# The change of x2 from token rows to feature rows for batches 2 to 5: TensorE turns replaced by 32 by 32 block turns and transfers

## What is computed

```python
x = _layernorm(x + _L0_attn_ref(x, Wq, Wk, Wv, Wo))      # causal self-attention, 16 heads, rotary
x = _layernorm(x + _L0_xattn_ref(x, ctx_4096))           # softmax(x ctx^T) ctx
x = _layernorm(x + _L0_ffn_ref(x, weight, bias, lora_A, lora_B, lora_start_indices))  # x W^T + bias + LoRA by batch
```

## Time and profile before

| | before |
|---|---|
| median of 3 runs (lowest, highest) | 523.33 us (523.15, 524.16) |
| the profiled execution, its own time | 522.58 us |
| its span, first to last instruction | 520.6 us |
| PE busy | 513.0 us, 99% of the span |
| PEld, DVE, ACT, POOL busy | 438.4, 319.8, 262.6, 152.1 us |
| granted TensorE clock, mean | 0.996 of full speed |
| DMA, all 16 engines | 65.60 MB, mean 126 GB/s |

### The profile page before, as it was taken

How to read it: one execution, slowest core, us unless ns; L and a number is a source line. 1 busy time by engine, 2 the same in 40 slices (tenths; PEclk the granted TensorE clock), 3 DMA queues, 4 the chain that set the end, 5 groups by cost and what they waited for, 6 DMA issues and landing times.

```text
span 520.6 us, 7823 instructions
## 1 busy us (share of the span) xinstructions
PE 513.0 (99%) x2864; PEld 438.4 (84%) x2864; DVE 319.8 (61%) x693; ACT 262.6 (50%) x664; POOL 152.1 (29%) x139
## 2 busy tenths in 40 slices
PE   8999999999999999999999999999999999999995
PEld 5888888888989888888978888888887888988884
DVE  5822000187776868677674797769887776845432
ACT  5713210183856648384565356357868464525231
POOL 0003500536353554742006150113937000110010
PEclk9999999999999999999999999999999999999998
DMA  8907612331021111100095677579987477333011
GB/s 284 320 16 180 184 40 82 126 118 51 32 69 55 42 40 43 42 2 0 1 280 162 146 205 210 148 200 262 263 247 212 133 207 214 104 91 110 1 75 47
DMA packets 37958, 65.60 MB, mean 126 GB/s; under 512 B 4872, under 2 KB 20616, under 8 KB 37920
## 3 DMA queue, kind: packets, MB, share of 16 engines
q1 hardware_dynamic: 37248, 64.58, 43.1%
q10 hardware_dynamic: 672, 0.52, 0.3%
HBM read 54.08 MB, written 3.67 MB: 111 GB/s over the span
## 4 chain that ended last, share of the span: by engine, by line
PE 98%; DMA 1%; ACT 0%; DVE 0%; SPq 0%; issue 0%; ACTq 0%
PE bank L539 30%; PE bank L656 30%; PE bank L550 15%; PE bank L742 6%; PE bank L566 3%; PE bank L581 3%; PE bank L773 2%; PE bank L775 2%; PE bank L778 2%; PE bank L726 1%; PE bank L715 1%; DMA x_raw<-x_feat 1%; PE bank L687 1%; PE bank L793 1%; PE bank L689 1%; PE bank L796 1%
## 5 line engine op out<-in xcount | busy, mean ns | idle before, releaser
L539 PE MATMUL bank<-x_hi,w_hi 128*128 128x512 f32 (+1 forms) x256 | 93.7, 366 | 0.0
L539 PE MATMUL bank<-x_hi,w_lo 128*128 128x512 f32 (+1 forms) x256 | 93.2, 364 | 0.0
L539 PE MATMUL bank<-x_lo,w_hi 128*128 128x512 f32 (+1 forms) x256 | 93.1, 364 | 0.0
L1386 DVE STREAM_TRANSPOSE prob_t<-prob 32x256 f32<-32x256 f32 x160 | 69.7, 436 | 12.1 <-ACT prob L947 9.4
L656 PE MATMUL bank<-wo,act_hi 128*128 128x512 f32 x224 | 70.2, 395 | 0.0
L656 PE MATMUL bank<-ffn,act_hi 128*128 128x512 f32 x224 | 70.0, 394 | 0.0
L1755 POOL TENSOR_TENSOR w_lo<-w_mix,w_hi 128x1024 fp32r<-128x1024 f32 x16 | 38.3, 2396 | 104.6 <-ACT w_hi L922 104.6
L937 ACT ACTIVATE prob<-prob,shift 112x112 f32<-112x112 f32 x128 | 47.8, 378 | 40.8 <-DVE shift L1369 40.8
L1768 POOL TENSOR_TENSOR norm<-norm,minus_half 128x1 f32<-128x1 f32 (+1 forms) x22 | 16.8, 765 | 156.5 <-DVE norm L1459 156.5
L539 PEld LDWEIGHTS bank<-x_hi,w_hi 128*128 128x128 f32 x256 | 48.1, 188 | 6.0
L539 PEld LDWEIGHTS bank<-x_lo,w_hi 128*128 128x128 f32 x256 | 48.1, 188 | 5.1
(11 more groups left out here) (119 smaller groups left out, 960.6 us busy)
## 6 DMA issues: line engine op xcount, KB each, us to landing
cf_raw<-ctx_feat SPq DMA_DIRECT2D x32, 376.0 KB, 4.1
ct_raw<-ctx_tok SPq DMA_DIRECT2D x24, 448.0 KB
w_raw<-qkv_w SPq DMA_DIRECT2D x16, 512.0 KB, 3.4
half_raw<-wo_w SPq DMA_DIRECT2D x16, 256.0 KB, 5.8
half_raw<-ffn_w SPq DMA_DIRECT2D x16, 256.0 KB, 7.0
wv_raw<-qkv_w SPq DMA_DIRECT2D x15, 256.0 KB, 7.2
x_raw<-x_feat SPq DMA_DIRECT2D x7, 448.0 KB, 8.1
out<-y_t SPq DMA_DIRECT2D x6, 512.0 KB, 3.9
```

The costliest lines, as they stand in the source:

```text
L539: last = pe.matmul(to[:, 0:cols.stop - cols.start], a[:, k, :], b[:, k, cols], start=(k == 0 and b is x_hi and a is w_hi[w]), stop=(k == K ...
L1386: return dve.transpose(quads(prob_t_wide[r], key, query), quads(prob_wide[r], query, key))
```

## The change

Batches 2 to 5 (`BLOCKS`) no longer pass through PE and PSUM. `swap_blocks(b)`: one DVE transpose of the whole row buffer in place, 128 partitions by 1024, which turns each 32 by 32 block by itself. `move_blocks(b, q)`: for 32 tokens (q = 0 to 3) four SP transfers, each of 32 partitions by 8 runs of 32 floats (16 for q = 3), carry the blocks to their feature partitions in `act_raw`, which lies on `act_lo`; four calls a batch make 16 transfers of 32 KB or less. `round_blocks(b)` on ACT waits for all 16 and writes `act_hi`, `rest_blocks(b)` on DVE writes `act_lo` in place. The row buffers get 16 rows more (112 to 127), set to zero once by POOL (`rows_set`) before the first `copy_row`. The order of the calls on SP, ACT, DVE and POOL is rewritten around this. Eight semaphores of `wv_in` become two, so `round_wv(1, k)` waits for four loads at a time.

```diff
-TURNS = ["a0", "a1", "a2", "b0", "a3", "b1", "a4", "b2", "a5", "b3", "a6", "b4", "b5", "b6", "b7"]
+TURNS = ["a0", "a1", "a2", "b0", "a3", "b1", "a4", "a5", "a6", "b6", "b7"]
+BLOCKS = range(2, 6)
...
+        act_raw = at("act_raw", [P, KT, B * S], A0 + 28672)
...
-        row = [at(f"row{i}", [S, D], (Q0 + 24576, S0 + 12288, S0 + 16384)[i]) for i in range(ROWS)]
+        row_all = [at(f"row{i}", [P, D], (Q0 + 24576, S0 + 12288, S0 + 16384)[i]) for i in range(ROWS)]
+        row = [r[0:S, :] for r in row_all]
...
             def copy_row(b, which):
                 if b >= ROWS:
-                    sp.wait_ge(turned, 2 * AT_TURN[f"b{b - ROWS}"] + 2)
+                    if b - ROWS in BLOCKS:
+                        sp.wait_ge(moved, 256 * blocks_before(b - ROWS) + 256)
+                    else:
+                        sp.wait_ge(turned, 2 * AT_TURN[f"b{b - ROWS}"] + 2)
...
+            def move_blocks(b, q):
+                sp.wait_ge(swapped, blocks_before(b) + 1)
+                if blocks_before(b):
+                    sp.wait_ge(moved, 256 * blocks_before(b))
+                t, n = b * S + QUAD * q, min(QUAD, S - QUAD * q)
+                for d in range(QUADS):
+                    sp.dma_start(act_raw[QUAD * d:QUAD * d + QUAD, :, t:t + n],
+                                 row_all[b % ROWS][QUAD * q:QUAD * q + QUAD, :].rearrange(
+                                     "p (k d i) -> p k d i", k=KT, d=QUADS)[:, :, d, 0:n]
+                                 ).then_inc(moved, 16)
...
             def ffn(i, n, turns=0):
...
+                if i + 1 in BLOCKS:
+                    pe.wait_ge(block_rest, 2 * blocks_before(i + 1) + 2)
+                else:
+                    pe.wait_ge(turn_rest, 2 * AT_TURN[f"b{i + 1}"] + 2)
...
-            turn_row(2)
-            turn_row(3)
-            turn_row(4)
-            turn_row(5)
...
+            def round_blocks(b):
+                act.wait_ge(moved, 256 * blocks_before(b) + 256)
+                for c in range(2):
+                    ks = slice(4 * c, 4 * c + 4)
+                    act.activation(act_hi[:, ks, tokens_of(b)], act_raw[:, ks, tokens_of(b)],
+                                   ACT.Copy).then_inc(block_rounded, 1)
...
+            def swap_blocks(b):
+                dve.wait_ge(x2_ready, b + 1)
+                dve.transpose(row_all[b % ROWS][:, :], row_all[b % ROWS][:, :]).then_inc(swapped, 1)
+            def rest_blocks(b):
+                for c in range(2):
+                    ks = slice(4 * c, 4 * c + 4)
+                    dve.wait_ge(block_rounded, 2 * blocks_before(b) + c + 1)
+                    dve.tensor_tensor(act_lo[:, ks, tokens_of(b)], act_raw[:, ks, tokens_of(b)],
+                                      act_hi[:, ks, tokens_of(b)].bitcast(F32),
+                                      ALU.subtract).then_inc(block_rest, 1)
```

More of the change, by code:

```diff
@@ L243, in build @@
         x_rounded, x_rest = sem("x_rounded"), sem("x_rest")
-        wv_in = [[sem(f"wv_in{c}_{k}") for k in range(KT)] for c in range(2)]
+        wv_in = [[sem(f"wv_in0_{k}") for k in range(KT)], [sem(f"wv_in1_{h}") for h in range(2)]]
         wv_rounded, wv_rest = sem("wv_rounded"), sem("wv_rest")
@@ L327, in load_wv @@
                              qkv_w[4 * c:4 * c + 4, 2, :, k, :].rearrange("s p f -> p s f")
-                             ).then_inc(wv_in[c][k], 16)
+                             ).then_inc(wv_in[0][k] if c == 0 else wv_in[1][k // 4], 16)
             def load_w(s, w):
@@ L458, in _ @@
             load_x(6)
+            load_ff(0)
+            load_ff(1)
             load_cf(14)
+            load_ff(2)
+            load_ff(3)
             load_ct(2, 0)
@@ L462, in _ @@
             load_ct(2, 2)
-            load_ff(0)
-            load_ff(1)
-            load_ff(2)
-            load_cf(15)
-            load_ff(3)
-            load_cf(16)
             load_ff(4)
-            load_cf(17)
-            copy_row(4, 0)
             load_ff(5)
@@ L474, in _ @@
             load_ff(7)
+            load_cf(15)
+            load_cf(16)
+            load_cf(17)
+            copy_row(4, 0)
             copy_row(4, 1)
@@ L480, in _ @@
             load_ff(8)
+            load_ff(9)
+            load_ff(10)
             load_cf(19)
-            load_ff(9)
+            load_ff(11)
+            move_blocks(2, 0)
+            move_blocks(2, 1)
+            move_blocks(2, 2)
+            move_blocks(2, 3)
+            load_ff(12)
             load_cf(20)
+            load_ff(13)
             load_cf(21)
-            load_ff(10)
+            load_ff(14)
+            load_cf(22)
+            load_ff(15)
             copy_row(5, 0)
             copy_row(5, 1)
-            load_ff(11)
-            load_ff(12)
-            load_ff(13)
-            load_ff(14)
-            load_ff(15)
-            load_cf(22)
             load_ct(4, 0)
@@ L499, in _ @@
             load_cf(25)
+            move_blocks(3, 0)
+            move_blocks(3, 1)
+            move_blocks(3, 2)
+            move_blocks(3, 3)
+            load_cf(26)
             copy_row(6, 0)
-            copy_row(6, 1)
-            load_cf(26)
             load_ct(5, 0)
@@ L505, in _ @@
             load_ct(5, 2)
-            store_y(0)
+            copy_row(6, 1)
             load_cf(27)
+            move_blocks(4, 0)
+            move_blocks(4, 1)
+            move_blocks(4, 2)
+            move_blocks(4, 3)
             load_cf(28)
             load_cf(29)
+            load_cf(30)
             copy_row(7, 0)
-            store_y(1)
-            load_cf(30)
+            store_y(0)
             load_ct(6, 0)
@@ L924, in round_wv @@
             def round_wv(c, k):
-                act.wait_ge(wv_in[c][k], 16)
+                if c == 0:
+                    act.wait_ge(wv_in[0][k], 16)
+                else:
+                    act.wait_ge(wv_in[1][k // 4], 64)
                 act.activation(wv_hi[c][:, k, :], wv_raw[c][:, k, :], ACT.Copy).then_inc(wv_rounded, 1)
@@ L1153, in _ @@
             cross_exp(2)
+            round_ff(0)
+            round_turned("a3")
             round_cf(14)
-            round_turned("a3")
+            round_ff(1)
+            round_ff(2)
+            round_ff(3)
             round_ct(12)
@@ L1221, in _ @@
             cross_exp(5)
-            norm_y(0)
+            round_blocks(3)
             round_cf(26)
@@ L1254, in _ @@
             round_ct(41)
+            round_blocks(5)
             cross_exp(7)
@@ L1646, in _ @@
             rest_cf(18)
+            swap_blocks(2)
             rest_ct(18)
@@ L1710, in _ @@
             rest_ct(41)
+            rest_blocks(5)
             add_row(6)
@@ L1807, in _ @@
                 rest_wo(q)
+            pool.wait_ge(heads_done, 2 * PAIRS)
+            pool.wait_ge(wo_rest, 2 * NB)
+            for i in range(ROWS):
+                pool.memset(row_all[i][P - QUAD:P, :], 0.0).then_inc(rows_set, 1)
+                pool.wait_ge(rows_set, i + 1)
             power(0, 0, P)
@@ L1813, in _ @@
             power(0, 3, P)
-            power(1, 1, S)
             add_one(0)
@@ L1828, in _ @@
             rest_ff(7)
+            power(0, 5, P)
             power(1, 2, S)
```

154 lines of the change are left out of this document (81 added, 73 removed).

## The result

| | before | after |
|---|---|---|
| median of 6 runs (lowest, highest) | 523.24 us (522.48, 524.16) | 533.28 us (530.55, 535.66) |
| the profiled execution, its own time | 522.58 us | 534.34 us |
| its span | 520.6 us | 532.3 us |
| granted TensorE clock, mean | 0.996 | 0.992 |

The change makes the kernel slower: ratio 1.0193, 95% interval 1.0164 to 1.0222, or +10.0 us by the medians. The forecast was 528.2 with a range up to 533.0, so the direction was right, the size half of what came, and the range was missed by 0.3 us.

The account below looks back on a forecast made before the run. The prediction took PE, busy 99% of the span, to bound the kernel. Its terms, -3.1 + 2.7 + 0.8 + 1.3 + 3.2 = +4.9, gave 527.5 us profiled and 528.2 as median, with a range from 520.0 to 533.

Parts of the forecast that it names:

- The removal: Four `turn_row` calls leave PE, 0.70 us each plus 0.07 for the pair behind: -3.1 us.
- the four priced stalls: PE waits forecast at `ffn(1, 0)`, `add_low(0, 0)`, `cross_score(6)` and `ffn(3, 0)`: +2.7, +0.8, +1.3 and +3.2 us.
- Price of the chain: From first move issue to finished batch: 9.9 issuing on SP, 3.0 landing, 1.75 rounding and rest; 14.65 us.
- `ffn(1, 0)`: Batch 2 moved from 382.0, finished at 396.65, while PE arrives at 393.97: a new stall of +2.7 us.
- The earlier `load_ff(0)` to `(7)` are covered by PE's own work: Loads moved ahead cost nothing; if uncovered, `norm_x2(1)` is late for `turn_row(1)` by a microsecond or so.
- `add_low(0, 0)`: `keep_t_part(0)` on ACT stands behind `round_cf(22)`, whose load the moves delay: +0.8 us, anything from 0 to 2.
- `cross_score(6)`: On DVE `rest_blocks(3)` holds back `add_row(4)` and `rest_turned("a6")`, which PE needs there: +1.3 us.
- `ffn(3, 0)`: Batch 4 moved from 431.4, finished at 446.05, while PE wants it at 442.8: +3.2 us.
- The clock: Rival: PE's clock falls to half level after stalls of 2.7 and 3.2 us, 1.5 us each: 531, chance 0.08.
- the cheap issue: Rival: SP issues each move in 0.38 us like a load, PE waits nowhere: 520.2 us, chance 0.22.
- The transfer bound: Rival: transfers themselves limit; at 60 ns a run, 15.4 us a batch and about 538 us, chance 0.05.
- its doubled case: Transfers over 32 partitions reach only 8 of 16 ports, doubling 41 ns a run: 21 us a batch, some 550 us.

Follow-up runs that it names:

- Run 1: Changed kernel's order on every queue, but no blocks: batches 2 to 5 turned on PE again; 524.74 us, ratio 1.0034 to the kernel before.
- run 3: Changed kernel with 8 moves a batch in place of 16, half of x2's features left out; 522.45 us, ratio 0.9991 to the kernel before.
- run 9: Changed kernel with 9 and 12 idle matmuls ahead of `add_low(0, 0)` and `ffn(3, 0)`; 531.74 us, ratio 1.0168 to the kernel before.
- run 5: Changed kernel with each batch's 16 moves replaced by four stores to DRAM and one load; 525.71 us, ratio 1.0050 to the kernel before.
- run 7: Changed kernel with `keep_t_part(0)` on ACT put ahead of `round_cf(21)` and `round_cf(22)`; 532.75 us, ratio 1.0186 to the kernel before.
- run 2: Changed kernel, blocks kept, with SP, ACT, DVE and POOL order from `load_x(6)` to `load_cf(17)` as before; 533.25 us, ratio 1.0192 to the kernel before.
- run 10: Changed kernel with four stores and one load through DRAM a batch, early order as before, `load_cf(19)` and its rounding earlier; 526.35 us, ratio 1.0055.
- run 8: Changed kernel with batch 3's rounding on ACT and `rest_blocks(3)` on DVE moved later, behind `add_row(4)`; 530.74 us, ratio 1.0135 to the kernel before.

## Why the prediction came out as it did

The removal came close to its term, and so did two of the four priced stalls. The other two missed in opposite directions, 2.7 against 0.30 and 0.8 against 2.50, so that the four together came to 7.1 us where the forecast had 8.0: that is luck. What failed is what stood at nothing in the sum: the reordered loads ahead of the blocks, and the clock behind the long waits. The forecast was +4.9 and the profiled execution showed +11.7; of the 6.8 between them the waits without a term make 3.5 and the half clock 3.2.

- **Removed**, -3.1: measured -2.8, 0.70 for each call; the 0.07 for the pair behind it didn't come.
- **Price of the chain**, 14.65 us: from 384.0 to PE's start at 397.68 it took 13.7. An issue at 0.66 was right (10.48 / 16 = 0.655), the swap at 1.3 too (1.246), landing at 3.0 was high (1.9).
- **`ffn(1, 0)`**, +2.7: measured 0.30, and PE there 2.94 later than before where I had 1.9. The chain was 1 us shorter but started at 384.0 and not at 382.0: the swap ended 1.0 late, at 382.9, and SP was not through with `load_ff(8)` to `(11)`, as the prediction had it, but issued them from 381.70 to 383.95, since they follow PE. And PE was late by itself.
- **"The earlier `load_ff(0)` to `(7)` are covered by PE's own work"**: this step failed, a term put at nothing without a row. Up to `ffn(1, 0)` the trace has 2.3 us of waits behind `cf_lo` and `ct_lo`: 1.33 and 0.42 ahead of the first move, and 0.53 at `cross_score(4)`, where the order alone has none. Up to the first move the kernels of runs 1, 3 and 9 have the same order and waited 0.83, 1.71 and 0.81 there, so one execution fixes this only to about 1 us. I had looked at the margin of the loads that were pulled ahead, and not at that of `load_cf(15)` to `(19)`, which they were put in front of. The victim I named, `turn_row(1)`, has no wait in this trace; in runs 5 and 7 it waits for 0.46 and 0.72. Run 1 prices the order at 1.6, and runs 2 and 10 show that with the blocks it can't simply be undone.
- **`add_low(0, 0)`**, +0.8: the place and the mechanism are right (`keep_t_part` at 405.05 behind `round_cf(22)`), the size 2.50: this term was mis-sized. `keep_t_part(0)` came 2.7 us later than the 402.35 I had, 1.9 of it because SP ended the moves late, while PE was only 1.0 later than I had it. I hadn't carried SP's lateness from term to term, only PE's.
- **`cross_score(6)`**, +1.3: 1.07. **`ffn(3, 0)`**, +3.2: 3.27. Both as worked out in size, and run 8 shows the mechanism.
- **The clock**: it stood among the rivals, at 0.08, with 1.5 us for each long wait. This is the other step that failed: it is no rival but a term, since it comes on top of stalls that the forecast itself has (2.7 and 3.2 us). It took 1.5 and 1.7. With it the forecast's own sum would have been 531.2; run 9 shows that it can be had back in part.
- **The rivals**: the cheap issue is out (0.611 measured, 0.601 with half the load). The transfer bound is out (share 0.33 and 0.37 where little else moves), and so are the 21 us a batch of its doubled case: 16 transfers were issued in 10.5 to 11.3 us and landed 1.9 us after their issue. The prediction took that doubling from 8 of 16 ports for 32 partitions (the Trainium skill, "SBUF — State Buffer", Door 1); at this rate of issue nothing of it is seen.

## What to carry to other kernels

On a kernel in which one engine is never idle, a step that leaves it for a queue is paid by the number of issues: here 16 issues of 0.65 us to save 0.70 us of PE. Ask first which loads stand behind them, and which roundings stand behind those loads on other engines; with half the issues the loss was gone, with half the bytes it was not. Each engine's order is a queue of this kind, not only SP's: the swap held back DVE (runs 2 and 10), and POOL's weight work held back ACT (run 7). Waits that such a queue sets come back at another place when one of them is mended. So a term of such a sum has to carry the queue's lateness along, a wait as long as those that dropped the clock has to be priced with what follows it, and before a wait is mended its trace has to say whether the load or the engine behind it was late.
